# Router results for two chunks at a time, and step zero's first layer and masks moved between the last chunk's attention

## The reference

```python
x = x + _L0_xattn_ref(_layernorm(x), ctx_1024, ...)   # attention by shifts (FFT)
x = x + _L0_ffn_ref(_layernorm(x), ...)               # weights composed from 32 low-rank parts, gelu
x = x + _L1_xattn_ref(_layernorm(x), ctx_1024, ...)   # softmax attention, one head, 128 keys per sequence
x = x + _L1_ffn_ref(_layernorm(x), ...)

# _L1_ffn_ref, per token
logits = _gelu(xf @ w_r1 + b_r1) @ w_r2 + b_r2        # 8 experts
top_p, top_i = jax.lax.top_k(softmax(logits), 2)      # two of them, weights normalized
for _ in range(2):
    ctx = concatenate([integrated, v])
    shared_ctrl = _gelu(ctx @ w_s1 + b_s1) @ w_s2 + b_s2
    hidden = _gelu(ctx_e @ w1[expert] + b1[expert]); ctrl = hidden @ w2[expert] + b2[expert]
    # alpha, beta, gate from ctrl; x_next, v_next as weighted sums of the shared and the routed state
    halt = sigmoid(_gelu(x_next @ w_h1 + b_h1) @ w_h2 + b_h2)
    refined = _gelu(x_next @ w_f1 + b_f1) @ w_f2 + b_f2
    integrated = integrated + halt * refined * integration_weight
    v = v_next
```

## Time and profile before

| | us |
|---|---|
| median of 3 runs | 358.88 (358.85 to 359.8) |
| the profiled execution, its own time | 360.02 |
| its span in the trace | 358.2 |
| PE busy | 327.9 (92%) |
| DVE busy | 284.2 (79%) |
| ACT busy | 196.2 (55%) |
| mean granted clock of PE | 0.981 of full speed |

### The profile page before, as it was taken

The page is one execution under the profiler, slowest core; times in us unless marked ns, Lnnn a source line. Parts: engine busy times, 40 slices in busy tenths (PEclk is TensorE's granted clock), DMA queues, the critical chain, the costliest instruction groups (busy, mean ns, idle before and its releaser), DMA issues.

```text
span 358.2 us, 4385 instructions
## 1 busy us (share of the span) xinstructions
PE 327.9 (92%) x1513; PEld 231.5 (65%) x1521; DVE 284.2 (79%) x598; ACT 196.2 (55%) x309; POOL 21.1 (6%) x24
## 2 busy tenths in 40 slices
PE   4989999899888889599798999999999999999996
PEld 4754787445454557367476677777777777777663
DVE  0556767655768777979997999999997997999694
ACT  2500025385637285186876686775855846734744
POOL 0040020202010112000000100000000000000000
PEclk9989999999999999789899999999999999999999
DMA  7999920000000000000000010100100100000001
GB/s 248 425 424 298 333 124 0 0 4 0 0 0 2 1 0 2 0 0 3 1 0 2 5 24 0 31 0 2 30 0 3 29 0 2 29 0 0 31 0 59
DMA packets 11445, 18.92 MB, mean 53 GB/s; under 512 B 416, under 2 KB 8864, under 8 KB 10144
## 3 DMA queue, kind: packets, MB, share of 16 engines
q1 hardware_dynamic: 10848, 17.60, 14.3%
q0 software_dynamic: 576, 1.05, 1.7%
HBM read 16.55 MB, written 1.05 MB: 49 GB/s over the span
## 4 chain that ended last, share of the span: by engine, by line
PE 70%; DVE 19%; issue 4%; ACT 3%; POOL 3%; DMA 2%; SPq 0%; DVEq 0%; ACTq 0%; POOLq 0%
PE ps L1200 65%; DVE zz L803 4%; POOL lrs L359 3%; DVE lst L788 2%; DMA ctxT<-in_ctxT 2%; PE ps L1297 1%; PE ps L1383 1%; PE ps L1276 1%; DVE lmv L791 1%; DVE st L688 1%; ACT hid L484 1%; PE ps L1371 1%; DVE a L704 1%; DVE lve L793 1%; DVE ctxT L1090 0%
## 5 line engine op out<-in xcount | busy, mean ns | idle before, releaser
L1200 PE MATMUL ps<-hm_odd,ew_hi 128*128 128x512 f32 (+1 forms) x164 | 52.3, 421 | 0.0
L1200 PE MATMUL ps<-hm_even,ew_hi 128*128 128x512 f32 (+1 forms) x160 | 49.7, 414 | 0.0
L1200 PEld LDWEIGHTS ps<-hm_odd,ew_hi 128*128 128x128 f32 (+1 forms) x164 | 29.1, 191 | 6.5 <-issue 0.5
L1200 PEld LDWEIGHTS ps<-hm_even,ew_hi 128*128 128x128 f32 (+1 forms) x160 | 27.5, 188 | 5.2
L1200 PE MATMUL ps<-hm_odd,ew_lo 128*128 128x512 f32 (+1 forms) x80 | 28.8, 397 | 0.0
L1200 PE MATMUL ps<-hm_even,ew_lo 128*128 128x512 f32 (+1 forms) x80 | 28.0, 390 | 0.0
L484 ACT ACTIVATE hid<-ps,pB 128x512 f32<-128x512 f32 x32 | 21.7, 687 | 10.4 <-PE ps L1200 9.7
L1200 PE MATMUL ps<-x_hi,w1x_hi 128*128 128x512 f32 x40 | 20.1, 503 | 5.7 <-ACT hid L484 3.9
L803 DVE TENSOR_SCALAR zz<-ps,lmv,lrs 128x128 f32<-128x128 f32 x48 | 16.4, 405 | 7.7 <-POOL lrs L359 7.5
L897 DVE SCALAR_TENSOR_TENSOR ring<-ring,pB,hid 128x1024 f32<-128x1024 bf16 x16 | 20.5, 1283 | 0.9
L788 DVE BATCH_NORM_STATS2 lst<-ps 128x6 f32<-128x128 f32 x48 | 10.7, 285 | 11.9 <-PE ps L1276 11.8
(11 more groups left out here) (286 smaller groups left out, 740.0 us busy)
## 6 DMA issues: line engine op xcount, KB each, us to landing
ring<-in_fc1b SPq DMA_DIRECT2D x4, 1024.0 KB, 17.8
ring<-in_fc2a SPq DMA_DIRECT2D x4, 1024.0 KB, 9.0
packC<-in_packC SPq DMA_DIRECT2D x1, 1152.0 KB, 9.2
pB<-in_packB SPq DMA_DIRECT2D x1, 1141.5 KB, 10.1
ctxT<-in_ctxT SPq DMA_DIRECT2D x2, 512.0 KB, 6.6
xtok<-in_xtok SPq DMA_DIRECT2D x1, 1024.0 KB, 9.2
xT<-in_xT SPq DMA_DIRECT2D x1, 1024.0 KB, 11.2
a<-in_fc1a SPq DMA_DIRECT2D x1, 1024.0 KB, 13.2
```

Source lines behind the costliest of these rows:

```text
L1200: return pe.matmul(out, lhsT, rhs, start=start, stop=stop)
```

## The change

- `route` and `weigh` always treat two chunks. The copy of the logits into `lg` is a function of its own, `logits(c)`. `route(0)` stands behind slot 3 and finds the experts of chunks 0 and 1, `route(2)` stands behind the last of the attention for chunks 2 and 3; `weigh(0)` and `weigh(2)` likewise, the latter in step 2's `hidden_masked`.
- The loop of slots ends with slot 3. What slots 4 and 5 held is written out: the attention of chunks 2 and 3 and the router of 2 and 3 alternate with step zero's hidden tiles (order 1, 2, 0, 3, 4, in banks 2 and 3) and their masks on DVE.
- Chunk 3's router stands inside step zero's controls on PE, behind their fourth tile and behind the group.
- `expand`, `expand_weights` and their copies for chunks 2 and 3, and the weights of 0 and 1, stand inside the controls of steps 0, 1 and 2; before, only four of the eight stood there. `slot_masks(1)` stands in the last chunk's attention, `slot_masks(2)` and `(3)` at the end of `hidden_masked(1)` and `(2)`.
- 23 matmuls that nobody reads are gone: 7 of `busy` and 2 and 14 of `FILL`.
- The router of chunk 3 gets bank 1, and the control groups swap their banks (group 0 in 3 to 5).

```diff
-            for t in range(SLOTS):
-                f, a, q, x = (0 <= t - i < NCH for i in range(4))
+            for t in range(NCH):          # DVE
+                a, q = t >= 1, t >= 2
...
-                if f:
-
-                    ln_stats("att", t)
-                if q and t < SLOTS - 1:
-                    route(t - 2)
-                if f:
-                    ln_scale("att", t)
+                ln_stats("att", t)
+                ln_scale("att", t)
+                if q:
+                    logits(t - 2)
+            route(0)
+
+            att_add(2)
+            ln_stats("rt", 2)
+            att_max(3)
+            slot_masks(0)
+            ln_scale("rt", 2)
+            kept(0, 1)
+            att_norm(3)
+            lower(0, 1)
             kept(0, 2)
-            lower(0, 1)
+            att_pt(3)
+            lower(0, 2)
+
+            att_add(3)
+            logits(2)
+            slot_masks(1)
+            ln_stats("rt", 3)
+            lower(0, 0)
             kept(0, 3)
+            ln_scale("rt", 3)
+            lower(0, 3)
+            shared_halves(0)
             state_split(1)
-            lower(0, 2)
-            shared_halves(0)
-            lower(0, 3)
-            route(NCH - 1)
+            weigh(0)
+            logits(3)
+            route(2)
...
                 kept(s, 1)
-                if s == 1:
-                    weigh(NCH - 2, 2)
                 kept(s, 2)
+                if s == 2:
+                    weigh(2)
...
                 lower(s, 3)
+                if s <= 2:
+                    slot_masks(s + 1)
...
-            FILL = {("att", 0): 5, ("att", 1): 4, ("att", 2): 9, ("rt", 2): 2, ("rt", 3): 14}
+            FILL = {("att", 0): 5, ("att", 1): 4, ("att", 2): 9}
...
+            att_v(2)                      # PE
+            ln_zt("att", 3)
+            q_proj(3)
+            pe.wait_ge(sem("fh"), FT * NCH)
+            expand(0, 2, 3)
+            ln_tok("rt", 2, "x3")
+            scores(3)
+            hidden(0, (1, 2))
+            ln_zt("rt", 2)
+            hidden(0, (0, 3))
+            probs_t(3)
+            router1(2)
+            hidden(0, (HT,))
+            router2(2)
+            att_v(3)
...
+            expand(1, 3, 2)
+            ln_tok("rt", 3, "x3")
...
+                    controls(0, BETA, between={5: routed})
+                    router2(3)
+                    hidden(1)
+                    controls(0, GATE, between={2: weights_0, 4: expand_2})
+                    continue
...
+                controls(s, BETA, between={1: {2: expand_3, 5: weights_1}, 2: {3: weights_2, 6: weights_3}}.get(s, {}))
...
+            z_att(3)                      # ACT
+            q_evac(3)
+            expand_evac(0, 2, 3)
+            exps(3)
+            second_exp(0)
+            hidden_gelus(0, (1, 2))
+            ln_evac("rt", 2, xi[:, ck(2)])
+            hidden_gelus(0, (0, 3))
+            r1_gelu(2)
+            hidden_gelus(0, (HT,))
+            expand_evac(1, 3, 2)
+            ln_evac("rt", 3, xi[:, ck(3)])
+            r1_gelu(3)
```

More of the change, by code:

```diff
@@ L1003, in _ @@
             weights_low()
-            for t in range(SLOTS):
-                f, a, q, x = (0 <= t - i < NCH for i in range(4))
+            for t in range(NCH):
+                a, q = t >= 1, t >= 2
                 if t + 2 < NCH:
@@ L1011, in _ @@
                     ln_scale("ffn", t + 2)
-                if x and not f:
-                    slot_masks(t - 3)
                 if q:
                     ln_stats("rt", t - 2)
-                if t == SLOTS - 1:
-                    kept(0, 1)
-                    lower(0, 0)
                 if a:
@@ L1024, in _ @@
                     att_norm(t - 1)
-                if x and f:
-                    slot_masks(t - 3)
-                if x and t < SLOTS - 1:
-                    weigh(t - 3)
-                if f:
-                    ffn_add(t)
+                ffn_add(t)
                 if t == 2:
@@ L1452, in _ @@
                     att_v(t - 2)
-                if t == SLOTS - 1:
-                    hidden(0, (2,))
-                if x and not f:
-                    pe.wait_ge(sem("cb"), 2 * (t - 3))
-                    busy(7 if t == SLOTS - 2 else 0, bank[2])
-                    expand(t - 3, 2, 3)
-                if t == SLOTS - 1:
-                    hidden(0, (3,))
                 if a:
                     ln_zt("att", t - 1)
-                if f and t:
+                if t:
                     ffn_up(t, (2,))
@@ L1497, in _, with controls @@
                     router1(t - 2)
-                if x and t < SLOTS - 1:
-                    expand_weights(t - 3, 2, 3)
-                if f:
-                    ln_tok("att", t, "x2")
+                ln_tok("att", t, "x2")
                 if q:
                     router2(t - 2)
-                if t == SLOTS - 2:
-                    hidden(0, (1,))
-            pe.wait_ge(sem("z"), 3 * NCH)
-            pe.wait_ge(sem("x3"), NCH)
-            pe.wait_ge(sem("x2"), NCH)
+            att_v(2)
[13 more added lines that the diff above has]
+            att_v(3)
+            pe.wait_ge(sem("hid"), HT)
+            pe.wait_ge(sem("hsu"), 1)
+            expand(1, 3, 2)
+            ln_tok("rt", 3, "x3")
             pe.wait_ge(sem("bp"), 1)
             pe.wait_ge(sem("ew2_lo"), 2)
-            def controls(s, part, before=None, between=None):
+            def controls(s, part, before=None, between={}):
                 c = s % NCH
@@ L1517, in controls @@
                 o = slice(part * D, (part + 1) * D)
-                sh, lo, hi = (bank[3 * (n % 2) + k] for k in range(3))
+                sh, lo, hi = (bank[3 * ((n + 1) % 2) + k] for k in range(3))
                 top, bot = slice(0, 64), slice(64, 128)
```

263 lines of the change are left out of this document (137 added, 126 removed).

## The result

The changed kernel takes 364.07 us in the median of 4 runs (363.93 to 364.68), the kernel before 359.34 beside it. The ratio is 1.0135, 95% interval 1.0113 to 1.0157: the change makes the kernel slower by 4.7 us. The forecast was 356.6 in a range up to 360.0; both the sign and the range were wrong, and of the cases only the third rival lies on this side.

What follows compares the result with a forecast made beforehand. PE was taken as the bound from step 3's hidden tiles on. Full-clock gain 4.6 less 2.1 for clock and 0.2 for hand-overs gives 2.3 us; 358.88 - 2.3 = 356.6 us, range for 8 in 10 353.9 to 360.0.

Steps and rivals of the forecast that it cites:

- Slot 3 starts earlier: Start of slot 3: scaling no longer waits for the search, so PE's transposes start at 101.6, not 102.89; gain 1.3 us.
- slot 3 gets shorter: Slot 3 up to chunk 3's scaling: 4.0 us of waits, transposes and search go; scaling at 115.6, gain 5.3 us.
- the search: Chunk 3's chain: the two-chunk search, 3.2 us with scaling and copy, pays part back; step zero's first mask at 127.1.
- DVE then runs without a wait: Step zero's masks: DVE works 18.3 us unbroken to 145.4; step 1's first mask at 151.4, not 157.25; gain 5.9 us.
- Step 1 to step 3: From step 1's first mask: `stepped(0)` at 164.8, `hidden(3)` at 187.4, tiles 4.5 us, transposes 1.9; full-clock gain 4.6 us.
- The clock: Thin PE stretches ahead of path work: one low stretch costs 1.6 us, a second half of 1.0; 2.1 us lost.
- the low clock lasts beyond 5 us at a time: Sign named in advance, for PE's clock: if seen in the timeline after, the forecast is wrong.
- Rival 3: From 143.6 to `hidden(2)`: clock stays low through step zero, 8 us lost, time 362.3 us; chance 0.13.
- Rivals 2 and 4: Hand-overs between 115 and 152 eat 2.0 us: 358.6, chance 0.22; two ACT table loads cost 2.6 more: 359.2, chance 0.03.
- The base: Whole kernel: starting time of 358.88 us, the median of the runs, from which the gain was subtracted.
- the 354.3 said for a full clock: First rival: the clock stays full where the path runs, gain 4.6 us, 354.3 up to 355.5; chance 0.17.

Runs made afterwards that it cites:

- e1: The changed kernel with 45 matmuls for nobody put back into PE's waits: 356.75 us, ratio 0.9933.
- e12: The changed kernel, unaltered, run again on another chip: median 362.92 us, ratio 1.0120.
- e4: The kernel before with only the attention's scaling moved ahead of the search on DVE in slots 2 and 3: 362.48 us, ratio 1.0088.
- e5: e1 with the next step's slot masks moved ahead of the last split: 355.20 us, ratio 0.9882.
- e7: e1 with `expand(3)` and chunk 1's weights ahead of `hidden(2)` replacing nine fillers, chunk 2 and 3 weights and `weigh(2)` in step 1: 356.15 us.
- e9: e5 and e7 together: 355.04 us, ratio 0.9881.
- e10: e9 with only `expand(3)` ahead of `hidden(2)`, the weights of chunks 1, 2 and 3 in step 1's first controls: 354.48 us, ratio 0.9869.

## Why the prediction was wrong

- **Slot 3 starts earlier, slot 3 gets shorter, the search**: right. PE's transposes of slot 3 came at 101.26 (101.6 said). The scaling of chunk 3 came at 115.54 (115.6 said), the search for two chunks took 3.2 (3.2 said).
- **DVE then runs without a wait**: nearly right at full clock. e1 has the last split at 141.65 + 1.23 = 142.9 (143.6 said), and there too DVE waited once, 0.57 for ACT. In the kernel after it waited 1.37 for PE, right behind a low stretch, and 0.71 for ACT.
- **Step 1 to step 3**: right within 0.4 up to `hidden(3)` (187.75 in e1 for 187.4). PE idles ahead of `hidden(2)` for 3.77, about 4 was said. Two terms were mis-sized: the tiles took 5.0, not 4.5, since a gelu (0.66 us of wait) still stands between them, and the transposes cost 2.2, not 1.9. `hidden(3)` itself was 0.3 late. So the profiled gain at full clock is 360.02 - 356.56 = 3.5, not 4.6; by the medians (359.21 and 356.75) it is 2.5.
- **The clock**: this is the step that failed. It took "I take 1.6" for one low stretch "of the 175 kind", half of 1.0 for a second and nothing for a third: 2.1. There were five, and they cost 6.8 by the traces (7.3 by the medians of after and e1). The price of a low microsecond was even too high (0.46 said, 6.8 of 24 measured, 0.28). What was missed is how many there are and how long they last. The walk named thin stretches at 115.5 to 120, at 139.5 to 143.5 and ahead of `hidden(2)`, and a low stretch came with or behind each. It did not look for one between 124 and 132, where PE waits 1.52 us for DVE, 1.02 for nothing that the trace names ("issue") and 0.78 for ACT, nor at the 1.76 that it waits for the gelus of `hidden(1)` behind 155. And it took the length of a low stretch from the one at 175 in the earlier trace rows, 3.4 us. Those at 117.4 and 144.8 lasted 6.8, and they began with transposes and single matmuls between waits. The kernel before had one as long itself, the one at 148 in the earlier trace rows, which stays low to 155.3 (0.59 from 152 to 156). That was the sign "the low clock lasts beyond 5 us at a time" in the trace that the forecast was made from.
- **Rival 3**, 0.13, had the mechanism: it asked for more than 5.7 us lost, and 6.8 were. But half of this, 3.4, was lost ahead of its place, which began at the end of step zero's last split, and what was lost inside it would not have been enough. That its 362.3 comes nearest is in part luck. Of the reasons against it, "the full clock was back within 5 us" did not hold for the stretches at 117.4 and 144.8. The Trainium skill, "TensorE: Matmul & The Clock Gate", section "What's actually happening", has the low clock as the default that activity has to lift; the prediction said that by this rule its sum would come nearer to this rival, and set it aside. Rows of after agree with the rule: just ahead of or at the start of each of the five stretches PE waits, for 1.72, 0.78, 2.82, 1.76 and 3.77 us, and none stands behind a dense one.
- **Rivals 2 and 4**: no sign of either in e1's marks up to `hidden(3)`, which leave no room for 2.0 us of hand-overs. In after a table load on ACT at 154.80 takes 1.28 us and the gelu starts at 156.09, so no drain is seen here either.
- **The base**: the median of 3 that the forecast started from, 358.88, was low. Fifty further timings of the kernel before gave medians of 359.2 to 359.7. With that, the 354.3 said for a full clock becomes 355, and with the 1.1 that the traces show as mis-sized 356, where e1 measured 356.75; the last 0.8 no run explains. Of the 7.5 us between forecast and result the clock is thus about 5, the gain at full clock 2 and the base 0.5.

What stays open is why a given stretch falls low in one run of the same text and not in the next; the runs show that it does, not by what. So the 7.3 us are those of after's four runs, all at 0.961 or 0.962; e12's four, from 360.00 to 364.99, would give between 3 and 8.

## What to carry to other kernels

Where a change moves work from a dense engine's queue into waits of others, write PE's timeline as it will be, wait by wait, and count every thin piece ahead of work on the path; matmuls for nobody belong to an order, and when the order changes they have to be placed anew, not dropped. Moving one step earlier on one engine gains only if the next engine's queue has its consumer in front. Before an effect of a few us is put down to an edit, compare runs at the same mean clock.

## What the runs showed of the hardware

- Matmuls for nobody, 45 of 0.23 us, put only into PE's waits, are worth 7.3 us of 364 here, more than the whole order gains at full clock (2.5 us).
- The same text runs at several mean clocks on one chip, in steps: e4 at 0.986, 0.976 and 0.967 took about 360.4, 362.5 and 364.8 us. So 0.01 of mean clock, which is 7 us at half the clock (0.01 x 2 x 361), costs 2.3 us, a third of them. The eight timings of the kernel after spread over 5 us, those of each filled version (e1, e5, e7, e9, e10) over 0.6 to 1.4: filling PE's waits seems to make the time more repeatable too.
- Shifting work earlier can lower the clock: e4 moved nothing but one DVE step, and in its profiled run the stretch from 124 to 128 went from full clock to 0.50. It need not: three of its nine runs had a mean clock of 0.986, above the kernel before.
